# Latent attention loop: key rotation moved from GpSimd to VectorE, and TensorE's order between score units changed

## Chip, cores and metric

One core of one Trainium2 chip. The metric is the device time of one execution of the whole program in microseconds (us). TensorE does matrix products, VectorE and ScalarE elementwise work and reductions, GpSimd elementwise work, SyncE issues DMAs. In the rows they stand as PE (PEld its weight loads), DVE, ACT, POOL and SP.

## What is computed

A decoder of two layers on 32 sequences of 56 tokens of width 256. The change touches one phase of layer 0, the cross attention over a latent context of 1500 rows of width 64 per sequence ("batch"), with 16 heads:

```
kv_rope = kv_c * cos + rotate_half(kv_c) * sin           # 1500 x 64 per batch
scores  = q_r . k_r      (both projected; the kernel folds the weights into the queries)
attn    = softmax(scores)
ctx_c   = attn @ kv_rope                                  # then two output projections
```

Here `rotate_half` swaps the two halves of the 64 columns and negates one; the kernel has the sign in its sine table.

## The kernel before, in words

`latent_attention` first makes the queries of all batches, then runs one loop over the 32 batches (`B`), each engine with its own copy of the loop (`body(b, par)`, where `par` is the parity of `b`) and semaphores between them. The 1500 rows lie as 12 tiles (`KT`) of 125 rows (`KP`). All 16 heads times 56 tokens are 896 columns, held as two halves of 448.

For one batch the work is as follows.

- SyncE loads the raw rows (`raw`, two buffers), spreads the queries, and moves the softmax denominators out and their reciprocals back (`spread_reciprocals`: spread `den` to `den7`, send `rec7`, broadcast it to `rD`).
- GpSimd rotates the rows: `raw*cos` into `rot` (L2395), two half-width products with the sine table into `rot2` (L2397, L2400), their sum into `rot` (L2403), and the low half-precision part of the keys into `kk` (L2409), after ScalarE has written the high part (`high`, L2547). ScalarE also copies `rot` to `kv` (`rows`, L2553), which TensorE reads as the values.
- TensorE transposes the keys in two turns (`turn`, L2442): tiles 0 to 7 of batch b+1 in the last third of body b, tiles 8 to 11 of batch b in its first third. ScalarE copies each turn out of bank 7 (`evacuate`, L2538).
- TensorE makes 12 score units (`scores`, L2477), numbered n = 0 to 11. A unit is three pairs of matmuls into one of three double banks, so unit n waits for the exponential of unit n-3. ScalarE turns each into exponentials in `Pb` (L2588, "exp n").
- TensorE multiplies the exponentials with the values (`values`, L2455), accumulating in bank 6. VectorE adds the 12 tiles of exponentials up into `dsum` (L2638 the first, L2643 the ten others; "sum tt", tt = 1 to 11). TensorE sums `dsum` over the partitions (`denominators`, L2465, bank 7).
- ScalarE copies bank 6 to `pv` (`keep_context`, L2559, at n = 4 of the next body) and bank 7 to `den` (`keep_denominators`, L2565). `pv` is one buffer: `keep_context(b)` waits for `ct_made` to reach b, that is, for VectorE to have used up the previous batch's. VectorE takes the reciprocals (L2624) and scales the context by them (`context`, L2628).

The order on TensorE is written out by hand. Each body has three thirds, g = 0, 1, 2. A third is four score units (4g to 4g+3), then a turn (g = 0 and g = 2), then four tiles of values (g = 0 takes the last four tiles of the batch before), and at g = 0 the denominators of the batch before come after the values. In each engine's loop a wait holds back everything behind it on that engine.

VectorE's order before: sum 1 to 6, the reciprocals of the batch before, sum 7 to 10, the context of the batch before, sum 11. ScalarE's: exp 0 to 3, the second turn's copy, `high` of the next batch, `keep_context` of the batch before, exp 4, `keep_denominators`, exp 5 to 7, `rows` of the next batch, exp 8 to 10, the next batch's first turn copy, exp 11.

Of the kernel before, what the change touches and what calls it, by code (L numbers as in the profile page):

```python
# [2201 lines left out]
def latent_attention(nc, k, t, weights):  # L2202


    with ExitStack() as ctx:
# [62 lines left out]
        with ExitStack() as main:  # L2268
# [16 lines left out]
            raw = sb("raw", [KP, 2, KT, DC], c=main)  # L2285
            rot, rot2 = sb("rot", [KP, 2, KT, DC], c=main), sb("rot2", [KP, KT, DC], c=main)
            kv = sb("kv", [KP, 2, KT, DC], c=main)
# [21 lines left out]
            ones = sb("ones", [KP, DC], c=main)  # L2309
            own_pool = sem("pool")  # L2310
            raw_in = [sem("even_rows_loaded"), sem("odd_rows_loaded")]
            kv_made, kT_done, kT_made = sem("kv_made"), sem("kT_done"), sem("kT_made")
            rotated, kh_made, kl_made = sem("rows_rotated"), sem("kh_made"), sem("kl_made")
# [6 lines left out]

            NTURN = 2

# [3 lines left out]
            with nc.Block() as block:  # L2326
# [51 lines left out]
                @block.gpsimd  # L2378
                def _(pool):
                    s = Steps(pool, own_pool)  # L2380
                    nc.gpsimd.tensor_copy(B16[:, :, 0, :], Bs[:]).then_inc(bh_made, 1)
                    pool.wait_ge(bh_made, 1)
                    nc.gpsimd.tensor_tensor(B16[:, :, 1, :], Bs[:], B16[:, :, 0, :],
                                            ALU.subtract).then_inc(bl_made, 1)
                    pool.wait_ge(tables, 32)
                    Q = DC // 2

                    def body(b, par):
                        r = raw[:, par]

                        pool.wait_ge(raw_in[par], half_count(b, par))
                        if past(b, 2):

                            pool.wait_ge(kv_made, b - 1)
                        s(nc.gpsimd.tensor_tensor(rot[:, par], r, cosK[:], ALU.mult))  # L2395
                        s.settle()
                        s(nc.gpsimd.tensor_tensor(rot2[:, :, 0:Q], r[:, :, Q:DC], sinK[:, :, 0:Q],  # L2397
                                                  ALU.mult))
                        s.settle()
# [3 lines left out]
                        nc.gpsimd.tensor_tensor(rot[:, par], rot[:, par], rot2[:],  # L2403
                                                ALU.add).then_inc(rotated, 1)
                        pool.wait_ge(rotated, b + 1)
                        pool.wait_ge(kh_made, b + 1)
                        if past(b, 2):
                            pool.wait_ge(kT_done, (b - 1) * NTURN)
                        nc.gpsimd.tensor_tensor(halves(par, True), paired(rot[:, par]),  # L2409
                                                halves(par, False), ALU.subtract).then_inc(kl_made, 1)  # L2410
                        pool.wait_ge(kl_made, b + 1)

                    over_tiles(pool, body, 0, s, 3, n=B)

                @block.tensor
                def _(pe):
# [30 lines left out]
                    def values(b, par, tt):  # L2447
                        pe.wait_ge(exp_done, b * KT + (tt // 2 * 2 + 2))
                        if tt == 0:
                            pe.wait_ge(kv_made, b + 1)  # L2450
                        if tt == 0 and past(b, 1):
# [32 lines left out]
                    def body(b, par):  # L2484
# [8 lines left out]
                        for g in range(3):  # L2493
                            if g == 0:
                                pe.wait_ge(kT_made, b * NTURN + 1)
                                pe.wait_ge(spread[par], 4 * half_count(b, par))
                            if g == 2:
                                pe.wait_ge(kT_made, b * NTURN + 2)
                            for pair in (2 * g, 2 * g + 1):
                                for u in range(2):  # L2500
                                    scores(b, par, pair, u)
                            if g == 0:
                                turn(b, par, 1)
                            if g == 2 and live(b + 1, B):
# [19 lines left out]
                def _(act):  # L2524
# [18 lines left out]
                    def high(b, par):  # L2543
                        act.wait_ge(rotated, b + 1)
                        if past(b, 2):
                            act.wait_ge(kT_done, (b - 1) * NTURN)
                        nc.scalar.activation(halves(par, False), paired(rot[:, par]),  # L2547
                                             ACT.Copy).then_inc(kh_made, 1)

                    def rows(b, par):  # L2550
                        if past(b, 2):
                            act.wait_ge(pv_done, (b - 1) * KT)
                        nc.scalar.activation(kv[:, par], rot[:, par], ACT.Copy).then_inc(kv_made, 1)  # L2553

# [12 lines left out]
                    def body(b, par):  # L2567
                        if not live(b, B):
                            keep_queries(0)
                            high(0, 0)  # L2570
                            rows(0, 0)
                            with act.Fori(1, NG - 1) as g:
# [4 lines left out]
                        for n in range(KT):  # L2577
# [27 lines left out]
                def _(dve):  # L2605
# [21 lines left out]
                    def context(b, source):  # L2627
                        nc.vector.tensor_tensor(CT[:, ds(b, 1), :].rearrange("p o n -> p (o n)"),  # L2628
                                                source, rD[:], ALU.mult).then_inc(ct_made, 1)

                    def body(b, par):
                        for tt in range(1, KT):
                            dve.wait_ge(exp_done, b * KT + (tt // 2 * 2 + 2))
# [19 lines left out]
                    over_tiles(dve, body, 0, n=B)  # L2653
                    n = (B - 1) * DR
# [957 lines left out]
```

## Time and profile before

| what | value |
|---|---|
| median of 3 runs | 1872.93 us (1871.71 to 1884.01) |
| the profiled execution | 1873.22 us, of which 1871.5 us are the span of the profile |
| busy over the span | TensorE 1467.8 us (78%), VectorE 1393.7 us (74%), ScalarE 1068.7 us (57%), GpSimd 652.1 us (35%) |
| the latent loop | about 370 us to 981 us of the span |

A timeline row gives the start of an instruction (or of a run of like ones, with their count after the x) in us from the start of the span, the time it covers, the engine, the line of the kernel, what it writes and reads, and in brackets how long the engine had been idle before and what ended that. Successive instructions of an engine overlap a little, so a step is best read from start to start.

### The profile page before, as it was taken

The page shows a single profiled execution, that of the slowest core. Times are in us where ns is not written, and L with a number is a line of the kernel's source. Part 1 is how long each engine was busy: PE and PEld are TensorE (multiplying, and loading weights), DVE is VectorE, ACT ScalarE, POOL GpSimd, SP SyncE. Part 2 cuts the span into 40 slices and gives each one's busy share as a digit, 9 for nine tenths or more (in the row PEclk, how much of TensorE's full clock was granted, in tenths as well). Part 3 has the DMA queues.
Part 4 walks back from the last instruction along what each step waited for, and adds up shares of the span by engine and source line. Part 5 has one row for each costly group of instructions (what it writes and reads, how often), then busy time and mean ns, then how long its engine had stood idle before and what let it go on. Part 6 is the DMA issues. An engine that isn't in the chain of part 4 may idle for free. (4 is left out here: it accounts for less than half of the span.)

```text
span 1871.5 us, 40366 instructions
## 1 busy us (share of the span) xinstructions
PE 1467.8 (78%) x13805; PEld 930.2 (50%) x13820; DVE 1393.7 (74%) x2385; ACT 1068.7 (57%) x1820; POOL 652.1 (35%) x654
## 2 busy tenths in 40 slices
PE   1677776999999999999997466861687759956892
PEld 0455553444444444444447356761465547735782
DVE  6888874799999998888876773326789646667674
ACT  1777763777777776777763342431567435535461
POOL 1222212165555645454510254551333110027242
PEclk9655665999999999999998677985899779958896
DMA  6920000112212121212110153433000010024334
GB/s 157 332 104 1 1 1 33 37 34 56 60 46 69 46 67 49 63 53 64 52 26 2 40 159 121 136 109 109 1 1 0 1 26 1 0 87 135 100 106 157
DMA packets 93389, 123.67 MB, mean 66 GB/s; under 512 B 22945, under 2 KB 74217, under 8 KB 92867
## 3 DMA queue, kind: packets, MB, share of 16 engines
q1 hardware_dynamic: 83395, 98.88, 18.7%
q0 software_dynamic: 7776, 21.28, 3.2%
q10 hardware_dynamic: 2112, 2.10, 0.3%
q8 instruction: 67, 1.10, 0.2%
q14 instruction: 39, 0.32, 0.1%
HBM read 66.85 MB, written 40.30 MB: 57 GB/s over the span
## 5 line engine op out<-in xcount | busy, mean ns | idle before, releaser
L2643 DVE TENSOR_TENSOR lat_dsum<-lat_dsum,lat_Pb 125x896 f32<-125x896 f32 x320 | 481.5, 1505 | 43.0 <-ACT lat_Pb L2588 33.7
L2588 ACT ACTIVATE lat_Pb<-banks 125x896 f32<-125x896 f32 x384 | 329.2, 928 | 145.2 <-PE banks L2477 130.8
L2455 PE MATMUL banks<-lat_Pb,lat_kv 125*64 125x448 f32 x1536 | 306.5, 541 | 0.0
L2477 PE MATMUL banks<-lat_QH,lat_kT 64*125 64x448 f16 x1536 | 247.7, 363 | 5.0 <-DVE lat_QT L2613 2.1
L2477 PEld LDWEIGHTS banks<-lat_QH,lat_kT 64*125 64x125 f16 x1536 | 104.6, 133 | 139.3 <-issue 66.3
L2455 PEld LDWEIGHTS banks<-lat_Pb,lat_kv 125*64 125x64 f32 x1536 | 100.6, 137 | 146.4 <-issue 138.3
L2409 POOL TENSOR_TENSOR lat_kk<-lat_rot,lat_kk 125x768 f16<-125x768 f32 x32 | 66.9, 2090 | 265.3 <-ACT lat_kk L2547 265.3
L2978 POOL DMA_INDIRECT sent_outputs<-moe_yb,moe_yidx x98 | 99.4, 1014 | 135.9 <-ACT moe_yb L3235 107.7
L2477 PE MATMUL banks<-lat_QL,lat_kT 64*125 64x448 f16 x768 | 136.0, 351 | 0.0
L3116 PE MATMUL banks<-moe_w2d,moe_gT 88*128 (+3 forms) x780 | 106.1, 288 | 22.6 <-DVE moe_gT L3453 15.6
L3116 PEld LDWEIGHTS banks<-moe_w2d,moe_gT 88*128 88x128 f16 (+1 forms) x780 | 77.5, 103 | 39.6 <-issue 27.0
L3441 DVE COPY moe_xTb<-banks 128x1024 f16<-128x1024 f16 x49 | 33.8, 689 | 83.8 <-PE banks L3083 45.9
L2970 POOL DMA_INDIRECT sent_rows<-moe_arena,moe_idx x64 | 70.8, 1106 | 53.0 <-DVE moe_idx L3382 33.9
L3033 PE MATMUL banks<-moe_xTb,moe_w2i 128*88 128x256 f16 (+1 forms) x588 | 77.0, 282 | 13.0 <-DVE moe_xTb L3441 13.0
L2403 POOL TENSOR_TENSOR lat_rot<-lat_rot 125x768 f32<-125x768 f32 x32 | 80.0, 2501 | 2.5
L2395 POOL TENSOR_TENSOR lat_rot<-lat_raw,lat_cosK 125x768 f32<-125x768 f32 x32 | 69.7, 2179 | 29.0 <-DMA lat_raw<-in_ctx_dram 23.8
L3033 PEld LDWEIGHTS banks<-moe_xTb,moe_w2i 128*88 (+1 forms) x588 | 63.6, 115 | 19.6 <-issue 14.9
L1270 POOL TENSOR_TENSOR bit_vv<-bit_vf,bit_one 128x256 f16<-128x256 f32 x16 | 11.0, 689 | 163.8 <-PE banks L1557 153.3
L3194 ACT ACTIVATE moe_gT<-banks 88x512 f32<-88x512 f32 x37 | 21.9, 591 | 76.5 <-PE banks L3033 57.6
L2477 PEld LDWEIGHTS banks<-lat_QL,lat_kT 64*125 64x125 f16 x768 | 52.7, 134 | 10.3
L2638 DVE TENSOR_TENSOR lat_dsum<-lat_Pb 125x896 f32<-125x896 f32 x32 | 53.5, 1673 | 3.6 <-ACT lat_Pb L2588 3.6
L2397 POOL TENSOR_TENSOR lat_rot<-lat_raw,lat_sinK 125x384 f32<-125x384 f32 x32 | 54.5, 1704 | 2.5
(446 smaller groups left out, 3256.8 us busy)
## 6 DMA issues: line engine op xcount, KB each, us to landing
moe_xb<-sent_rows SPq DMA_DIRECT2D x49, 257.0 KB
lat_raw<-in_ctx_dram SPq DMA_DIRECT2D x32, 375.0 KB
sent_rows<-zero SPq DMA_DIRECT2D x1, 7453.0 KB, 49.0
lat_QH<-lat_QT SPq DMA_DIRECT2D x64, 112.0 KB, 2.9
lat_QL<-lat_QT SPq DMA_DIRECT2D x64, 112.0 KB, 5.0
lat_rD<-lat_reciprocals SPq DMA_DIRECT2D x62, 112.0 KB, 2.8
moe_arena<-sent_outputs SPq DMA_DIRECT2D x12, 512.0 KB, 6.5
sent_rows<-zero SPq DMA_DIRECT2D x1, 5140.0 KB, 65.1
```

The costliest lines, as they stand in the source:

```text
L2395: s(nc.gpsimd.tensor_tensor(rot[:, par], r, cosK[:], ALU.mult))
L2397: s(nc.gpsimd.tensor_tensor(rot2[:, :, 0:Q], r[:, :, Q:DC], sinK[:, :, 0:Q], ALU.mult))
L2403: nc.gpsimd.tensor_tensor(rot[:, par], rot[:, par], rot2[:], ALU.add).then_inc(rotated, 1)
L2409: nc.gpsimd.tensor_tensor(halves(par, True), paired(rot[:, par]), halves(par, False), ALU.subtract).then_inc(kl_made, 1)
L2455: ins = nc.tensor.matmul(ps[u * DC:(u + 1) * DC, 6, 0:8 * T], kv[:, par, tt, :], Pb[:, tile_slot(tt, par), u, :], start=tt == 0, stop=tt = ...
L2477: ins = nc.tensor.matmul(ps[0:KP, n % 3 * 2 + q, 0:8 * T], kT[rows, par, 2 * pair + low, 0:KP], Q[rows, par, 8 * u:8 * u + 8, :].rearrange ...
L2588: nc.scalar.activation(Pb[:, slot:slot + 2, u, :], ps[0:KP, n % 3 * 2:n % 3 * 2 + 2, 0:8 * T], ACT.Exp, scale=1.0 / QSCALE).then_inc(exp_d ...
L2643: ins = nc.vector.tensor_tensor(dsum[:, par], dsum[:, par], Pb[:, tile_slot(tt, par)], ALU.add)
L2970: nc.gpsimd.indirect_dma_start(xg[:, :], bass.IndirectOffsetOnAxis(ap=idx[:, c, i:i + 1], axis=0), rows[:, i, :], None).then_inc((sent0, s ...
L2978: nc.gpsimd.indirect_dma_start(ytok[:, :], bass.IndirectOffsetOnAxis(ap=yidx[:, n, h:h + 1], axis=0), yb[:, n % 3, h, :], None).then_inc(y ...
L3033: ins = nc.tensor.matmul(ps[0:FP, dst, j * BN:(j + 1) * BN], w[:, u, c, j * FP:(j + 1) * FP], rhs(v, c), start=a + c == 0, stop=a == 2 and ...
L3116: ins = nc.tensor.matmul(dst, gT2[:, n % 2, u, j, h * P:(h + 1) * P], w[:, v, j, :], start=a + j == 0, stop=last and not (gated and b < 0))
```

## The change

GpSimd rotates only the rows of batches 0 and 1, before the loop. For the others VectorE does it: it makes the three products of batch b+2 at the end of body b (`row_products`), adds them straight into `kv` after sum 3 of body b+1 (`rotated_rows`; the values of two batches earlier must have been used), and makes the low part after sum 7 (`low`). ScalarE's copy `rows` is gone; `high` reads `kv` and comes after exp 5 instead of exp 3. On TensorE the two turns and the denominators are put ahead of the last score unit of a third instead of behind the third, and the denominators move from g = 0 to g = 1. ScalarE keeps the denominators after exp 7 and VectorE takes their reciprocals after sum 9. The context of batch b-2 is scaled after sum 3 of body b, behind the rotation's sum; `keep_context` on ScalarE is unchanged. After the loop VectorE scales the context of batch 30 before its last checks.

The diff, cut to its core:

```
                 @block.tensor
-                            for pair in (2 * g, 2 * g + 1):
-                                for u in range(2):
-                                    scores(b, par, pair, u)
+                            for pair, u in ((2 * g, 0), (2 * g, 1), (2 * g + 1, 0)):
+                                scores(b, par, pair, u)
                             if g == 0:
                                 turn(b, par, 1)
+                            if g == 1 and past(b, 1):
+                                denominators(b - 1, (par + 1) % 2)
                             if g == 2 and live(b + 1, B):
                                 turn(b + 1, (par + 1) % 2, 0)
+                            scores(b, par, 2 * g + 1, 1)
                             for tt in range(4 * g - 4, 4 * g):
...
-                            if g == 0 and past(b, 1):
-                                denominators(b - 1, (par + 1) % 2)
                 @block.scalar
                             if n == 3:
                                 evacuate(b, par, 1)
-                                if live(b + 1, B):
-                                    high(b + 1, (par + 1) % 2)
-                            if n == 7 and live(b + 1, B):
-                                rows(b + 1, (par + 1) % 2)
-                            if n == 4 and past(b, 1):
+                            if n == 5 and live(b + 1, B):
+                                high(b + 1, (par + 1) % 2)
+                            if n == 7 and past(b, 1):
                                 keep_denominators(b - 1)
                 @block.vector
+                    def kept_context(b):
+                        dve.wait_ge(pv_kept, b + 1)
+                        dve.wait_ge(rec_in, 32 * b + 32)
+                        context(b, pv[:])
+                    def row_products(b, par):
+                        r = raw[:, par]
+                        dve.wait_ge(raw_in[par], half_count(b, par))
+                        dve.wait_ge(rotated, b)
+                        nc.vector.tensor_tensor(rot[:], r, cosK[:], ALU.mult)
+                        nc.vector.tensor_tensor(rot2[:, :, 0:Q], r[:, :, Q:DC], sinK[:, :, 0:Q], ALU.mult)
+                        nc.vector.tensor_tensor(rot2[:, :, Q:DC], r[:, :, 0:Q], sinK[:, :, Q:DC], ALU.mult)
+                    def rotated_rows(b, par):
+                        dve.wait_ge(products_made, 3 * b - 3)
+                        dve.wait_ge(pv_done, (b - 1) * KT)
+                        nc.vector.tensor_tensor(kv[:, par], rot[:], rot2[:], ALU.add).then_inc(rotated, 1)
+                    def low(b, par):
+                        dve.wait_ge(kh_made, b + 1)
+                        nc.vector.tensor_tensor(halves(par, True), paired(kv[:, par]),
+                                                halves(par, False), ALU.subtract).then_inc(kl_made, 1)
                     def body(b, par):
...
-                            if tt == 6 and past(b, 1):
+                            if tt == 3 and past(b, 1) and live(b + 1, B):
+                                rotated_rows(b + 1, other)
+                            if tt == 3 and past(b, 2):
+                                kept_context(b - 2)
+                            if tt == 7 and past(b, 1) and live(b + 1, B):
+                                low(b + 1, other)
+                            if tt == 9 and past(b, 1):
                                 reciprocals(b - 1)
-                            if tt == KT - 2 and past(b, 1):
-                                dve.wait_ge(pv_kept, b)
-                                dve.wait_ge(rec_in, 32 * b)
-                                context(b - 1, pv[:])
+                        if live(b + 2, B):
+                            row_products(b + 2, par)
+                    kept_context(B - 2)
```

On GpSimd, the loop over all batches becomes `for b in range(2)` with the same five instructions, the sum written to `kv[:, b]`.

## Rows read from the trace of the kernel before

**Rows 1.** The page's granted TensorE clock in 40 slices of the span

```profile
PEclk9655665999999999999998677985899779958896
```

**Rows 2.** ScalarE's copies of the context, one per batch: durations, first and last start

```profile
L2559 ACT ACTIVATE lat_pv<-banks x31: 543/543/547, 392.7 to 965.6; 128x448 f32<-128x448 f32 x31
```

**Rows 3.** Timeline of TensorE, one body from its g = 1 values on

```profile
819.56 3.23 PE L2455 MATMUL banks<-lat_Pb,lat_kv 125*64 125x448 f32 x16
...
825.30 0.63 PE L2442 MATMUL banks<-id,lat_kk 125*64 125x125 f16 x16
...
831.53 0.41 PE L2442 MATMUL banks<-id,lat_kk 125*64 125x125 f16 x8
831.78 3.18 PE L2455 MATMUL banks<-lat_Pb,lat_kv 125*64 125x448 f32 x16
834.79 0.92 PE L2465 MATMUL banks<-lat_dsum,lat_ones 125*64 125x448 f32 x4
835.64 0.40 PE L2477 MATMUL banks<-lat_QH,lat_kT 64*125 64x448 f16 x2
...
838.29 3.23 PE L2455 MATMUL banks<-lat_Pb,lat_kv 125*64 125x448 f32 x16
```

**Rows 4.** Timeline, all engines, of an earlier batch, where TensorE waits for VectorE

```profile
604.20 2.53 DVE L2638 TENSOR_TENSOR lat_dsum<-lat_Pb 125x896 f32<-125x896 f32 x1
604.42 0.97 PE L2465 MATMUL banks<-lat_dsum,lat_ones 125*64 125x448 f32 x4 [0.79 <-DVE lat_dsum L2643]
```

**Rows 5.** The sums on VectorE over the loop (group by line: total busy us, mean ns)

```profile
L2643 DVE TENSOR_TENSOR lat_dsum<-lat_dsum,lat_Pb 125x896 f32<-125x896 f32 x320 | 481.5, 1505 | 43.0 <-ACT lat_Pb L2588 33.7
```

**Rows 6.** Timeline of TensorE near the loop's end: four score units and the turn behind

```profile
959.63 0.40 PE L2477 MATMUL banks<-lat_QH,lat_kT 64*125 64x448 f16 x2
959.87 0.35 PE L2477 MATMUL banks<-lat_QL,lat_kT 64*125 64x448 f16 x2
960.06 0.54 PE L2477 MATMUL banks<-lat_QH,lat_kT 64*125 64x448 f16 x4
...
961.85 0.35 PE L2477 MATMUL banks<-lat_QH,lat_kT 64*125 64x448 f16 x2
962.13 0.41 PE L2442 MATMUL banks<-id,lat_kk 125*64 125x125 f16 x8
```

**Rows 7.** Timeline, exp 4 and what follows it on ScalarE and TensorE

```profile
836.61 0.92 ACT L2588 ACTIVATE lat_Pb<-banks 125x896 f32<-125x896 f32 x1 [0.98 <-PE banks L2477]
837.42 0.54 ACT L2565 ACTIVATE lat_den<-banks 128x448 f32<-128x448 f32 x1
837.58 0.13 PEld L2477 LDWEIGHTS banks<-lat_QH,lat_kT 64*125 64x125 f16 x2 [0.43 <-ACT lat_Pb L2588]
837.85 2.54 ACT L2588 ACTIVATE lat_Pb<-banks 125x896 f32<-125x896 f32 x3
```

**Rows 8.** Timeline, exponentials and the sums that wait for them, GpSimd idle

```profile
954.37 2.54 ACT L2588 ACTIVATE lat_Pb<-banks 125x896 f32<-125x896 f32 x3 [1.16 <-PE banks L2477]
...
956.22 2.22 DVE L2643 TENSOR_TENSOR lat_dsum<-lat_dsum,lat_Pb 125x896 f32<-125x896 f32 x2 [0.75 <-ACT lat_Pb L2588]
958.74 1.09 DVE L2643 TENSOR_TENSOR lat_dsum<-lat_dsum,lat_Pb 125x896 f32<-125x896 f32 x1 [0.30 <-ACT lat_Pb L2588]
959.75 0.62 DVE L2628 TENSOR_TENSOR lat_QT<-lat_pv,lat_rD 128x448 f32 x1
```

**Rows 9.** Timeline: a reciprocal and the context behind it, then the loop's tail

```profile
616.64 0.19 DVE L2624 RECIPROCAL lat_rec<-lat_den 128x7 f32 x1
...
621.94 0.63 DVE L2628 TENSOR_TENSOR lat_QT<-lat_pv,lat_rD 128x448 f32 x1 [0.72 <-DMA lat_rD<-lat_reciprocals]
...
971.90 0.40 PE L2477 MATMUL banks<-lat_QH,lat_kT 64*125 64x448 f16 x2
...
979.37 0.27 DVE L2657 TENSOR_SCALAR lat_good<-lat_rec 128x217 f32<-128x217 f32 x1
...
981.51 2.96 DVE L2665 RECIPROCAL lat_rD<-banks 128x448 f32<-128x448 f32 x1 [1.04 <-PE banks L2465]
```

More of the change, by code:

```diff
@@ L2285, in latent_attention @@
             raw = sb("raw", [KP, 2, KT, DC], c=main)
-            rot, rot2 = sb("rot", [KP, 2, KT, DC], c=main), sb("rot2", [KP, KT, DC], c=main)
+            rot, rot2 = sb("rot", [KP, KT, DC], c=main), sb("rot2", [KP, KT, DC], c=main)
             kv = sb("kv", [KP, 2, KT, DC], c=main)
@@ L2309, in latent_attention @@
             ones = sb("ones", [KP, DC], c=main)
-            own_pool = sem("pool")
+            own_pool, products_made = sem("pool"), sem("row_products_made")
             raw_in = [sem("even_rows_loaded"), sem("odd_rows_loaded")]
-            kv_made, kT_done, kT_made = sem("kv_made"), sem("kT_done"), sem("kT_made")
+            kT_done, kT_made = sem("kT_done"), sem("kT_made")
             rotated, kh_made, kl_made = sem("rows_rotated"), sem("kh_made"), sem("kl_made")
@@ L2319, in latent_attention @@
                 sem("good_reduced"), sem("good_counted"))
-            NTURN = 2
+            NTURN, Q = 2, DC // 2
             def past(i, least=0):
@@ L2385, in _ @@
                     pool.wait_ge(tables, 32)
[L2386 to L2396, printed above, removed]
+                    for b in range(2):
+                        r = raw[:, b]
+                        pool.wait_ge(raw_in[b], 16)
+                        if b:
+                            pool.wait_ge(rotated, 1)
+                        s(nc.gpsimd.tensor_tensor(rot[:], r, cosK[:], ALU.mult))
                         s(nc.gpsimd.tensor_tensor(rot2[:, :, 0:Q], r[:, :, Q:DC], sinK[:, :, 0:Q],
                                                   ALU.mult))
-                        s.settle()
                         s(nc.gpsimd.tensor_tensor(rot2[:, :, Q:DC], r[:, :, 0:Q], sinK[:, :, Q:DC],
@@ L2402, in body @@
                         s.settle()
-                        nc.gpsimd.tensor_tensor(rot[:, par], rot[:, par], rot2[:],
-                                                ALU.add).then_inc(rotated, 1)
+                        nc.gpsimd.tensor_tensor(kv[:, b], rot[:], rot2[:], ALU.add).then_inc(rotated, 1)
                         pool.wait_ge(rotated, b + 1)
                         pool.wait_ge(kh_made, b + 1)
[L2407 to L2413, printed above, removed]
+                        nc.gpsimd.tensor_tensor(halves(b, True), paired(kv[:, b]), halves(b, False),
+                                                ALU.subtract).then_inc(kl_made, 1)
                 @block.tensor
@@ L2449, in values @@
                         if tt == 0:
-                            pe.wait_ge(kv_made, b + 1)
+                            pe.wait_ge(rotated, b + 1)
                         if tt == 0 and past(b, 1):
@@ L2546, in high @@
                             act.wait_ge(kT_done, (b - 1) * NTURN)
-                        nc.scalar.activation(halves(par, False), paired(rot[:, par]),
+                        nc.scalar.activation(halves(par, False), paired(kv[:, par]),
                                              ACT.Copy).then_inc(kh_made, 1)
[L2550 to L2553, printed above, removed]
                     def keep_context(b):
@@ L2570, in body @@
                             high(0, 0)
-                            rows(0, 0)
                             with act.Fori(1, NG - 1) as g:
@@ L2629, in context @@
                                                 source, rD[:], ALU.mult).then_inc(ct_made, 1)
+                    def kept_context(b):
[6 more added lines that the diff above has]
+                        dve.wait_ge(rotated, b)
+                        nc.vector.tensor_tensor(rot[:], r, cosK[:], ALU.mult).then_inc(products_made, 1)
+                        nc.vector.tensor_tensor(rot2[:, :, 0:Q], r[:, :, Q:DC], sinK[:, :, 0:Q],
+                                                ALU.mult).then_inc(products_made, 1)
+                        nc.vector.tensor_tensor(rot2[:, :, Q:DC], r[:, :, 0:Q], sinK[:, :, Q:DC],
+                                                ALU.mult).then_inc(products_made, 1)
+                    def rotated_rows(b, par):
+                        dve.wait_ge(products_made, 3 * b - 3)
+                        dve.wait_ge(pv_done, (b - 1) * KT)
+                        nc.vector.tensor_tensor(kv[:, par], rot[:], rot2[:], ALU.add
+                                                ).then_inc(rotated, 1)
+                    def low(b, par):
+                        dve.wait_ge(kh_made, b + 1)
+                        nc.vector.tensor_tensor(halves(par, True), paired(kv[:, par]),
+                                                halves(par, False), ALU.subtract).then_inc(kl_made, 1)
                     def body(b, par):
+                        if not live(b, B):
+                            return
+                        other = (par + 1) % 2
                         for tt in range(1, KT):
@@ L2645, in body @@
                             ins.then_inc(summed, 1)
-                            if tt == 6 and past(b, 1):
-                                reciprocals(b - 1)
-                            if tt == KT - 2 and past(b, 1):
-                                dve.wait_ge(pv_kept, b)
-                                dve.wait_ge(rec_in, 32 * b)
-                                context(b - 1, pv[:])
-                    over_tiles(dve, body, 0, n=B)
+                            if tt == 3 and past(b, 1) and live(b + 1, B):
[5 more added lines that the diff above has]
+                            if tt == 9 and past(b, 1):
+                                reciprocals(b - 1)
+                        if live(b + 2, B):
+                            row_products(b + 2, par)
+                    over_tiles(dve, body, 1, n=B)
+                    kept_context(B - 2)
                     n = (B - 1) * DR
```

## Prediction

> **What bounds the kernel now.** I read the page's slices first, for the phases and the granted clock: in the loop's slices TensorE holds its upper level, 2.4 GHz, with a 9 in each of them up to the last [rows 1]. So a matmul has one price there and the loop can be read as a pattern. Next the period. ScalarE's copy of the context runs once per body, and 31 of them span 965.6-392.7 = 572.9 us, 30 periods of 19.10 us [rows 2]. Then TensorE's timeline of one body. From values to the like values it takes 838.29-819.56 = 18.73 us [rows 3], with no gap in which TensorE waits long. Earlier bodies add a wait of up to 0.79 us before the denominators, for VectorE's last sum [rows 4], which makes the mean 19.10. VectorE is late there because a sum takes 1505 ns in the mean [rows 5] against 1.09 us where GpSimd is idle [rows 8]; one of 2.53 us stands in [rows 4]. So TensorE's own order is the floor, and VectorE, slowed beside GpSimd, adds 0.37 us per body. That is all the change can win from VectorE's relief, however many busy microseconds go.
>
> **TensorE's order, part by part.** A score unit is three pairs of matmuls, 0.19 us a pair (959.87 to 960.06); entering the scores costs 0.05 more (959.63 to 959.87 is 0.24) and leaving them 0.09 (961.85 to 962.13 is 0.28) [rows 6]. Twelve pairs with both edges are 2.41 us (with 0.1885 for a pair, before rounding). The same third takes 2.50 in [rows 6] and 838.29-835.64 = 2.65 us in [rows 3]: up to 0.24 us is the fourth unit's wait for the exponential three units back, with its restart. Four tiles of values cost 834.79-831.78 = 3.01 us between a turn and the denominators, and the denominators 835.64-834.79 = 0.85 for two pairs of 0.375, so leaving this kind of matmul for scores costs 0.10 [rows 3]. Values between scores then cost 3.01+0.05+0.10 = 3.16. A turn of 8 transposes costs 831.78-831.53 = 0.25 us, one of 16 about 0.47 (its record is 0.22 longer) [rows 3].
>
> In the new order each third is three units, the inserted work, one unit, values. Three units: 9 x 0.1885 + 0.14 = 1.84; the last unit 0.71. So g = 0 is 1.84+0.25+0.10+0.71+3.16 = 6.06 us; g = 1, with denominators of 0.75+0.05, is 6.61; g = 2 is 6.28. The sum is 18.95 us against 18.73: six more edge pairs of about 0.15 cost as much as the three waits give back, and a little more. I take the turn's exit to be the denominators' 0.10, the nearest row; its bounds are nothing and the 0.15 of a full edge, 0.2 us per body either way.
>
> The Trainium skill, TensorEngine Tiling (Array Packing), section Key Properties, says that a change of tiling mode (not only of tile) drains TensorE. Scores use 64 rows and the rest 125, and the rows' 0.05 to 0.10 us per edge agree. Without that rule one would book the three waits as pure gain.
>
> **VectorE and ScalarE.** VectorE loses nothing of its 11 sums (1.09 us each, 2.22-1.09 = 1.13 from one to the next) [rows 8]. It gains one sum and one low part of 768 columns and three products of 768, 384, 384. The trace has no such operation on VectorE: by its rows of 448 and 896 columns, 0.62 and 1.09 us [rows 8], 768 columns are 0.96 and 384 are 0.55 (bounds for 768: those two rows). That is 4.0 us, and with 12.3 of sums, the context and the reciprocal 17.1 us per body, under the period: VectorE isn't filled. ScalarE loses the 0.9 us copy and isn't filled either. GpSimd leaves the loop. The two ramps for which it still works (batches 0 and 1) I cost at nothing: batch 0's low part was ready long before the loop, and batch 1's turn comes over 5 us after the exponentials that its high part follows. SyncE's order is unchanged; the raw rows have more than half a body of slack, and its queue is released by the reciprocals as before.
>
> **The wait that the change builds.** `keep_context` of batch b-1 stands on ScalarE ahead of exp 4 of body b and waits until the context of batch b-2 is made. Before, VectorE had made that one in body b-1, so the wait cost nothing. Now it is made in the same body b, after sum 3 and behind the rotation's sum. Exp 4 to 11, `high` and both copies are queued behind `keep_context`. I walk one body. Times are from the start of g = 0.
>
> - Exp 0 starts 0.98 after the third's first unit (836.61 against 835.64), the next ones 0.81 apart [rows 3, 7]. Exp 3 starts at 3.41, and VectorE's sum 2, which waits for it, 1.04 later (0.92 and 0.12 of latency: 956.22 is 1.85 after the first of two exponentials) [rows 8]: 4.45. Sum 3 at 5.58. The rotation's sum at 6.59 (1.01 after a sum) [rows 8]; its own wait, for the values of g = 0, ends before, at about 6.25. The context at 7.47 (0.96 less the overlap of 0.08), done at 8.09.
> - `keep_context` starts at 8.21 and exp 4 at 8.64 (0.43 after a 0.54 copy: 837.42 to 837.85) [rows 7]. From the start of g = 1 (6.06) that is 2.58, where it used to be 0.98. The last unit of g = 1 may start 0.97 after exp 4 (836.61 to 837.58) [rows 7], at 3.55; the order alone would have it at 1.84+0.80+0.10 = 2.74. **First stall: 0.81 us.**
> - Exp 5 follows at 3.39 from the start of g = 1, `high` at 4.20, exp 6 at 4.90 (0.70 for `high`'s 768 columns, between the 0.43 and 0.81 that copies of 448 and 896 take to the next start [rows 7], which bound it), exp 7 at 5.71. Sum 6 waits for exp 7: 4.90+1.85 = 6.75. Sum 7 at 7.88, the low part at 8.89, done at 9.85. The turn of g = 2 waits for it: 9.98. g = 2 starts at 6.61+0.81 = 7.42 and would turn at 9.26. **Second stall: 0.72 us.** The denominators, once the late link, now have over 6 us to spare.
> - The sums 8 to 11 and the products end at 2.3 us into the next body, before exp 1 is there (2.7), so nothing more accumulates, and nothing is caught up.
>
> The period is 18.95+0.81+0.72 = 20.48 us. In which body it holds: from 2 to 30; body 1 has no context to wait for (18.97), and body 31 no rotation and no turn. Sum over the 30 periods: 29 x 20.48 + 18.97 = 612.9 us against 572.9, +40.0. For bodies 0 and 31, +0.2.
>
> **The tail.** The reciprocal of batch 30 now comes after sum 9, about 4.9 us into the last third, and the context waits for the DMAs behind it, 621.94-616.64 = 5.3 us [rows 9]: it runs at 10.2 to 10.85, three short checks (979.37 to 980.5, about 1.1 us) follow, and the reciprocal of L2665 starts near 11.9 after the last third's start. Before it was 981.51-971.90 = 9.6 [rows 9]: +2.3.
>
> **Sum.** 40.0+0.2+2.3 = +42.5. The profiled execution took 1873.2 us, 0.3 from the median of the runs shown, so both lead to 1916 us. The links of the chain are good to about 0.3 us a period, 9 us in all.
>
> **Rivals.**
>
> - One stall only (the turn's). If the low part is ready in time (a quicker `high`, or exp 7 not held as I think), the period is 19.76 and the time 1916-29 x 0.72 = 1895 us. For it: the two stalls are worked out in series and the second hangs on eleven links. Against: each link has its row. Chance 0.15.
> - The clock. Each body now has two idle stretches of TensorE of 0.75 us. In the earlier bodies, stretches of 0.79 [rows 4] left the granted clock at its upper level [rows 1]. If it falls to 1.2 GHz in some bodies, each such fall costs two to three microseconds by the time a third of scores takes at half rate (2.65 against twice that); eight of them give 1936. Chance 0.1.
> - Not slower: the context is made before `keep_context` wants it. It decides at 1.22 us after the start of g = 1 (2.74-0.97-0.43-0.12); I put it at 2.03. If VectorE is 0.8 us earlier, both stalls go, the period is 18.95, and the time is 1873-(572.9-29 x 18.95-18.97)+2.5 = 1871 us. For it: VectorE is much less busy. Against: sum 2 waits for exp 3, whose time TensorE and ScalarE set, and the wait for the values holds the rotation's sum until 6.25, so the chain can win 0.3 us at most. Chance 0.1.
> - Clearly faster: edges and waits both cheap, VectorE's relief counted in full. Period 18.73 less three waits of 0.24, 18.0: 1873-1.1 x 30+2.5, or 1843 us. The Trainium skill, SBUF — State Buffer, section Who interferes with whom, has VectorE and GpSimd lock each other out of one shared port pair, and here sums of 2.53 against 1.09 us agree; as a rule for the time it speaks for this case. Against: TensorE's floor and the wait built. Chance 0.05.
>
> The forecast has 0.6. The range, from 1892 (under one stall) to 1932 (0.6 us more per period), leaves out about 0.2. A measurement of this kernel tells about 1% from no change. The stalls, one or two, and the clock give slower; one stall at its low end touches 1%. Slower 0.84, within 1% 0.11, faster 0.05.
>
> **What would show it.** ScalarE's L2559 waiting for VectorE's context, 1 to 2 us each; exp 4 starting some 2.5 us after the first score unit of g = 1; 30 copies of the context 20.4 us apart; TensorE idle before the fourth unit of g = 1 and before the 16 transposes, and not before the denominators; sums of 1.09 us throughout. It is wrong if those copies are 19 us apart, or if TensorE waits in other places.

## The result and the profile after

The changed kernel takes 1918.24 us in the median of 4 runs (1915.18 to 1918.77), the kernel before 1872.32 us beside it. The ratio is 1.024, 95% interval 1.020 to 1.028. The forecast was 1916 us.

The page of the kernel after, its slices and its costliest groups in the loop (columns as before: count, busy us, mean ns, idle before and its releaser):

```profile
PEclk9665657999999999999998867995799879958896
...
L2652 DVE TENSOR_TENSOR lat_dsum<-lat_dsum,lat_Pb 125x896 f32<-125x896 f32 x320 | 350.8, 1096 | 116.7 <-ACT lat_Pb L2570 105.1
L2570 ACT ACTIVATE lat_Pb<-banks 125x896 f32<-125x896 f32 x384 | 329.3, 926 | 129.0 <-PE banks L2465 128.8
```

VectorE is relieved as the change meant it to be: a sum takes 1096 ns in the mean, against 1505 in [rows 5]. It is also idle far more, 116.7 us before those sums against 43.0, waiting for exponentials. The granted clock stays at its upper level through the loop, as in [rows 1]. So the time was not lost to VectorE's work, nor to the clock.

ScalarE's copy of the context, which answers to [rows 2] (durations in ns, first and last start):

```profile
L2542 ACT ACTIVATE lat_pv<-banks x31: 543/543/544, 393.2 to 1005.5; 128x448 f32<-128x448 f32 x31
```

The waits of the latent phase, 340 to 1030 us (who waited for whom, total us, times, longest):

```profile
ACT lat_pv L2542 <- DVE lat_QT L2608: 99.2, 30, 3.4
PEld banks L2465 <- ACT lat_Pb L2570: 64.7, 63, 1.5
...
PE banks L2465 <- ACT lat_Pb L2570: 19.8, 30, 0.7
PE banks L2430 <- DVE lat_kk L2634: 19.5, 29, 0.7
```

The 31 copies span 1005.5-393.2 = 612.3 us, where the forecast had 612.9 and the kernel before 572.9. The waits name the links. The copy waits 30 times for VectorE's context (it used to wait for TensorE's values); TensorE waits 30 times for an exponential and 29 times for the low part, 0.7 us each, and never for a sum before the denominators.

One period in the timeline, ScalarE, VectorE and TensorE, each engine's rows together. The third g = 0 starts at 610.29 and g = 1 at 616.35:

```profile
611.27 3.35 ACT L2570 ACTIVATE lat_Pb<-banks 125x896 f32<-125x896 f32 x4 [2.85 <-PE banks L2465]
618.41 0.54 ACT L2542 ACTIVATE lat_pv<-banks 128x448 f32<-128x448 f32 x1 [3.31 <-DVE lat_QT L2608]
618.85 1.72 ACT L2570 ACTIVATE lat_Pb<-banks 125x896 f32<-125x896 f32 x2
...
614.75 2.22 DVE L2652 TENSOR_TENSOR lat_dsum<-lat_dsum,lat_Pb 125x896 f32<-125x896 f32 x2 [0.54 <-ACT lat_Pb L2570]
616.88 0.95 DVE L2629 TENSOR_TENSOR lat_kv<-lat_rot 125x768 f32<-125x768 f32 x1
617.75 0.62 DVE L2608 TENSOR_TENSOR lat_QT<-lat_pv,lat_rD 128x448 f32 x1
...
605.86 0.63 PE L2430 MATMUL banks<-id,lat_kk 125*64 125x125 f16 x16 [0.67 <-DVE lat_kk L2634]
610.29 0.40 PE L2465 MATMUL banks<-lat_QH,lat_kT 64*125 64x448 f16 x2
616.35 0.40 PE L2465 MATMUL banks<-lat_QH,lat_kT 64*125 64x448 f16 x2
619.81 0.40 PE L2465 MATMUL banks<-lat_QH,lat_kT 64*125 64x448 f16 x2 [0.64 <-ACT lat_Pb L2570]
```

Read from 610.29: sum 2 at 4.46 us, the rotation's sum at 6.59, the context at 7.46, `keep_context` at 8.12, exp 4 at 8.56, the fourth unit of g = 1 at 9.52. The forecast had 4.45, 6.59, 7.47, 8.21, 8.64 and 9.61.

### The profile page after: what moved, and what is told of

Same layout as the page of the kernel before. It is cut to its first block and busy times, and to the rows that moved or that the text cites. A ratio compares the mean times of both kernels' runs of the same rounds, so it can differ in the third digit from the quotient of the medians.

```text
span 1916.0 us, 40187 instructions
## 1 busy us (share of the span) xinstructions
PE 1476.1 (77%) x13805; PEld 933.7 (49%) x13820; DVE 1355.4 (71%) x2535; ACT 1042.5 (54%) x1788; POOL 342.3 (18%) x504
## 5 line engine op out<-in xcount | busy, mean ns | idle before, releaser
L2652 DVE TENSOR_TENSOR lat_dsum<-lat_dsum,lat_Pb 125x896 f32<-125x896 f32 x320 | 350.8, 1096 | 116.7 <-ACT lat_Pb L2570 105.1
L3047 PEld LDWEIGHTS banks<-moe_xTb,moe_w2i 128*88 (+1 forms) x588 | 63.0, 114 | 19.7 <-issue 14.8
L2542 ACT ACTIVATE lat_pv<-banks 128x448 f32<-128x448 f32 x31 | 16.8, 543 | 100.7 <-DVE lat_QT L2608 99.2
L3097 PE MATMUL banks<-id,moe_xb 128*128 128x128 f16 x392 | 32.5, 230 | 26.7 <-DMA moe_xb<-sent_rows 26.7
L2526 ACT ACTIVATE lat_kT<-banks 128x1000 f16<-128x1000 f16 x64 | 52.8, 825 | 0.0
L2410 PE MATMUL banks<-lat_cols,lat_A 128*128 (+1 forms) x128 | 51.2, 562 | 1.1 <-DVEq L2587 1.1
L3224 ACT ACTIVATE moe_uT<-banks,moe_bug 128x256 f32<-128x256 f32 x56 | 23.5, 470 | 51.0 <-PE banks L3047 26.5
```

The source lines that it names most:

```text
L2410: ins = nc.tensor.matmul(ps[:, j % 4, 0:GN], A[:, c, 2 * j:2 * j + 2, :].rearrange("p h d -> p (h d)"), cols[:, c, ds(g * GN, GN)], start= ...
L2526: nc.scalar.activation(kT[:, par, 8 * c:8 * c + n, 0:KP], ps[:, 7, :].bitcast(F16)[:, 0:n * KS].rearrange("p (n k) -> p n k", n=n)[:, :, 0 ...
L2652: ins = nc.vector.tensor_tensor(dsum[:, par], dsum[:, par], Pb[:, tile_slot(tt, par)], ALU.add)
L3047: ins = nc.tensor.matmul(ps[0:FP, dst, j * BN:(j + 1) * BN], w[:, u, c, j * FP:(j + 1) * FP], rhs(v, c), start=a + c == 0, stop=a == 2 and ...
L3097: ins = nc.tensor.transpose(bank[:, a, h * P:(h + 1) * P], xb[:, b % XB, h, a * P:(a + 1) * P], id16[:])
```

## The experiments

The runs fell on different chips. On the chip of the first four experiments the kernel before takes 1847.38 us, 25 us less than in the result above, so times are compared as ratios and periods. In the traces most of that difference lies behind the loop: from its last check to the end of the span these four take 861 to 867 us, the kernel before 885 in its first trace.

**Taking the two stalls apart.** Four kernels, each the changed one with one or two edits. Exchange of the context and the rotation's sum:

```
+                            if tt == 3 and past(b, 2):
+                                kept_context(b - 2)
                             if tt == 3 and past(b, 1) and live(b + 1, B):
                                 rotated_rows(b + 1, other)
-                            if tt == 3 and past(b, 2):
-                                kept_context(b - 2)
```

> The changed kernel with two statements of VectorE exchanged: after sum 3 the context of batch b-2 comes ahead of the rotation's sum. Theory (keep_context waits for that context, and the low part for exp 7): exp 4 starts 1.7 us after g = 1 begins instead of 2.6, the fourth unit of g = 1 no longer waits, the turn of g = 2 still does (about 0.65 us); period 19.6 us, time about 1894 us. Rival (VectorE's 4 us of added work per body is what costs): the same work in another order, so no change, 1918 us. Rival (TensorE's six added mode edges cost): no change, 1918 us.

Measured: ratio to the kernel before 1.011 (1.006 to 1.016), against 1.024 for the full change in the result above. From its waits between 400 and 970 us:

```profile
ACT lat_pv L2542 <- DVE lat_QT L2608: 71.5, 29, 2.5
...
PE banks L2430 <- DVE lat_kk L2634: 15.6, 29, 0.6
```

The row of TensorE waiting on its matmuls for an exponential is gone; the turn's wait for the low part stays. ScalarE's copy still waits 2.5 us (counted from its last instruction), but that no longer costs TensorE anything. Its copies span 979.8-392.6 = 587.2 us, a period of 19.57 where 19.6 was expected. One of the two stalls went, and the wait of the other is a little shorter (15.6 us in 29 times is 0.54, against 0.67), because exp 4 and all behind it still start late, but less late.

The low part after sum 5:

```
-                            if tt == 7 and past(b, 1) and live(b + 1, B):
+                            if tt == 5 and past(b, 1) and live(b + 1, B):
                                 low(b + 1, other)
```

> The changed kernel with the low part after sum 5 instead of sum 7. Theory: the turn of g = 2 no longer waits, the fourth unit of g = 1 still waits 0.8 us; period about 19.7 us, time about 1897 us. Both rivals (VectorE's load, TensorE's edges): no change, 1918 us.

Measured: ratio 1.013 (1.008 to 1.018). The other stall went and the first stayed, by its waits between 400 and 970 us. Its copies span 590.8 us, 19.69 a period where about 19.7 was expected.

```profile
ACT lat_pv L2542 <- DVE lat_QT L2608: 96.7, 29, 3.4
...
PE banks L2465 <- ACT lat_Pb L2570: 19.2, 29, 0.7
```

Both edits at once:

> Both exchanges at once. Theory: no stall is left in the loop, the period is TensorE's own order, 18.95 us, and the time about 1875 us; the two gains add up. Rival (VectorE's load): 1918 us. Rival (edges cost more than 0.15 us each): the period stays clearly above 19.1 us without any wait of TensorE for another engine.

Measured: ratio 1.000 (0.995 to 1.005). The copies span 569.5 us, 18.98 us a period:

```profile
L2542 ACT ACTIVATE lat_pv<-banks x31: 543/543/544, 391.5 to 961.0; 128x448 f32<-128x448 f32 x31
```

A second buffer for the kept context instead, VectorE's order untouched:

```
-            rD, pv = sb("rD", [P, 8 * T], c=main), sb("pv", [P, 8 * T], c=main)
+            rD, pv = sb("rD", [P, 8 * T], c=main), sb("pv", [P, 2, 8 * T], c=main)
...
-                        if past(b, 1):
-                            act.wait_ge(ct_made, b)
-                        nc.scalar.activation(pv[:], ps[:, 6, 0:8 * T], ACT.Copy)
+                        if past(b, 2):
+                            act.wait_ge(ct_made, b - 1)
+                        nc.scalar.activation(pv[:, par], ps[:, 6, 0:8 * T], ACT.Copy)
```

> The changed kernel, VectorE's order untouched, with two buffers for the kept context, so that keep_context waits for the context of one batch earlier. Theory: the first stall goes, and with it the second (exp 7 is 0.8 us earlier and more); period 18.95 us, time about 1875 us. If the two stalls are independent: the second stays, about 1895 us. Rivals: 1918 us.

Measured: ratio 1.000 (0.995 to 1.005). The copies now wait for TensorE's values alone, and both stalls are gone although the low part still comes after sum 7 (waits between 400 and 940 us; the copies span 568.6 us, 18.95 a period):

```profile
ACT lat_pv L2542 <- PE banks L2443: 39.4, 28, 1.4
```

So the second stall isn't a cost of its own. It is the first one's delay of exp 4 handed on through exp 7 to the sums behind; either breaking the handing on or removing its head is enough. The load rival falls with all four runs: the VectorE work was the same in each, 4 us a body more than before.

**The two parts of the change by themselves.** VectorE's part, with TensorE's order, denominators and context as before (here the low part is after sum 5):

```
-                            for pair, u in ((2 * g, 0), (2 * g, 1), (2 * g + 1, 0)):
-                                scores(b, par, pair, u)
+                            for pair in (2 * g, 2 * g + 1):
+                                for u in range(2):
+                                    scores(b, par, pair, u)
...
-                            if tt == 3 and past(b, 2):
-                                kept_context(b - 2)
+                            if tt == KT - 2 and past(b, 1):
+                                kept_context(b - 1)
```

> One part of the change alone: VectorE rotates (products at the body's end, the rotation's sum after sum 3, the low part after sum 5), GpSimd is out of the loop and the copy of rows is gone, but TensorE's order, the denominators, the reciprocals and the context stand as in the kernel before. Theory: the period is the late one of the kernel before, 18.73 us in every body, with no wait before the denominators; 0.37 us less than its mean over 30 periods, so 11 us faster than the kernel before, ratio 0.994. Rival (VectorE's added 4 us cost by themselves): no faster than the kernel before.

Measured: ratio 0.998 (0.9965 to 0.9995). The period came as forecast; here are TensorE's rows of one body, to be laid beside [rows 3]:

```profile
651.09 0.92 PE L2453 MATMUL banks<-lat_dsum,lat_ones 125*64 125x448 f32 x4
...
660.34 0.63 PE L2430 MATMUL banks<-id,lat_kk 125*64 125x125 f16 x16
...
666.57 0.41 PE L2430 MATMUL banks<-id,lat_kk 125*64 125x125 f16 x8
666.82 3.18 PE L2443 MATMUL banks<-lat_Pb,lat_kv 125*64 125x448 f32 x16
669.83 0.92 PE L2453 MATMUL banks<-lat_dsum,lat_ones 125*64 125x448 f32 x4
```

From denominators to denominators 18.74 us, and 3.01 us of values ahead of them, so no wait for VectorE. The same holds over the whole loop: the copies of the context span 561.2 us, 18.71 a period. But the gain in time is 3.7 us (1861.8 against 1865.52), not 11. The period was right and the comparison wasn't.

The order part, with GpSimd rotating as before:

```
+                            if tt == 1 and past(b, 2):
+                                kept_context(b - 2)
-                            if tt == 6 and past(b, 1):
+                            if tt == 9 and past(b, 1):
                                 reciprocals(b - 1)
-                            if tt == KT - 2 and past(b, 1):
...
-                                context(b - 1, pv[:])
```

> The other part alone: TensorE's new order (turns and denominators ahead of the third's last score unit) with GpSimd rotating as before; the context of batch b-2 is made after sum 1, where ScalarE doesn't wait for it. Theory: period 18.95 us, six more mode edges against three waits of the fourth unit; no wait for VectorE before the denominators in spite of GpSimd, since they come later; 0.15 us a period less than the mean before, 2 us more in the tail: ratio 0.999. Rival (the inserted work hides the waits for nothing): period 18.0 to 18.3 us, ratio 0.985 to 0.99.

Measured: ratio 1.015 (1.013 to 1.017), a miss. The waits between 450 and 920 us say why:

```profile
ACT lat_pv L2559 <- DVE lat_QT L2628: 60.4, 24, 3.2
...
DVE lat_QT L2628 <- DMA lat_rD<-lat_reciprocals: 50.9, 24, 2.8
```

I had put the context so early that it waited for the reciprocals' DMA, and ScalarE waited for it again: the same chain with another head. TensorE waited for an exponential 28 times in the loop, most often for 0.5 us. To tell this from an effect of GpSimd, the same kernel with two buffers and the context after sum 3:

> e7_order_part_alone (TensorE's new order, GpSimd rotating) with two buffers for the kept context and the context made after sum 3, so that neither ScalarE nor VectorE waits for the reciprocals' DMA. Theory (e7 lost its 0.5 us a body to keep_context waiting for a context that waited for that DMA): period 18.95 us, ratio 0.997 to 1.003. Rival (GpSimd beside VectorE makes the new order slow by itself): period stays at 19.5 us, ratio about 1.015.

Measured: ratio 1.001 (0.999 to 1.003). GpSimd works and the sums are as slow as before (the group of the sums, then the copies of the context), and yet the period is TensorE's own order, since the denominators come later:

```profile
L2648 DVE TENSOR_TENSOR lat_dsum<-lat_dsum,lat_Pb 125x896 f32<-125x896 f32 x317 | 477.0, 1505 | 29.9 <-ACT lat_Pb L2588 21.1
```

```profile
L2559 ACT ACTIVATE lat_pv<-banks x31: 544/545/547, 393.4 to 962.0; 128x448 f32<-128x448 f32 x31
```

568.6 us over 30 periods are 18.95. The order part alone is worth nothing. By itself the new order is 0.22 us a body longer than the old one at its best (18.95 against 18.73): it saves three waits of the fourth unit, and pays for six more changes between the scores, which use 64 rows of TensorE, and the other matmuls, which use 125 ("changes of mode" from here on). What made up for that here is that the denominators no longer wait for a slowed sum.

**GpSimd put back beside the rotation.** The VectorE part alone, and per body five GpSimd instructions of the old shapes on tiles of their own:

```
+                    def beside(b, par):
+                        pool.wait_ge(exp_done, b * KT + 4)
+                        s(nc.gpsimd.tensor_tensor(g1[:], sinK[:], cosK[:], ALU.mult))
...
+                    over_tiles(pool, beside, 0, s, 5, n=B)
```

> The kernel of e6_vector_part_alone with the five GpSimd instructions of the old loop put back on tiles of their own, paced by exp 3 of each body, so that nothing waits for them. Theory (the two engines slow each other whatever the data): sums on VectorE go from 1.09 us back to about 1.5 us in the mean where the five run, VectorE needs over 19 us a body together with the rotation, and the time is above the kernel before, ratio 1.01 to 1.03. Rival (the old slowness came from waits on shared tiles): sums stay at 1.09 us, the time equals e6_vector_part_alone.

Measured: ratio 1.074 (1.071 to 1.076), above what I expected. The sums went back to 1495 ns in the mean though they share no tile with GpSimd. The group of the sums, a stretch of the timeline, and a row of the waits between 450 and 1020 us:

```profile
L2669 DVE TENSOR_TENSOR lat_dsum<-lat_dsum,lat_Pb 125x896 f32<-125x896 f32 x310 | 463.3, 1495 | 18.4 <-ACT lat_Pb L2587 10.9
```

```profile
749.59 5.20 DVE L2669 TENSOR_TENSOR lat_dsum<-lat_dsum,lat_Pb 125x896 f32<-125x896 f32 x2
755.58 2.21 DVE L2669 TENSOR_TENSOR lat_dsum<-lat_dsum,lat_Pb 125x896 f32<-125x896 f32 x2
...
748.68 2.54 POOL L2413 TENSOR_TENSOR lat_g<-lat_g,lat_g2x 125x768 f32<-125x768 f32 x1
```

```profile
ACT lat_kk L2552 <- DVE lat_kv L2646: 93.1, 25, 7.9
```

Two sums take 5.20 us beside GpSimd's and 2.21 us after. The excess over the expectation is in part again a chain: `high` on ScalarE waits for the rotation's sum, which stands behind the slowed sums, and every later exponential stands behind `high`. TensorE then stands still for up to 6.1 us at a time, and behind such a wait its granted clock falls to the lower level, 1.2 GHz: a row of four matmuls, 0.54 us before the wait, is 0.95 behind it. Two such rows, and then the loop in this kernel and in the VectorE part alone (stretch, its length, busy us and count of PE, PEld, DVE, ACT and POOL, granted clock, DMA share, GB/s):

```profile
757.39 0.63 PE L2482 MATMUL banks<-lat_QH,lat_kT 64*125 64x448 f16 x2 [4.81 <-ACT lat_Pb L2587]
...
758.19 0.95 PE L2482 MATMUL banks<-lat_QH,lat_kT 64*125 64x448 f16 x4
```

```profile
392.00:1096.00 704.00, 598.97 (x4444) 272.67 (x4444) 664.32 (x544) 399.42 (x511) 311.66 (x151) 0.93 0.18 44
```

```profile
389.00:950.00 561.00, 559.25 (x4442) 253.18 (x4440) 476.95 (x539) 393.73 (x510) 0.00 (x0) 1.00 0.22 56
```

For the same matmuls TensorE is busy 599.0 us against 559.3. So of the 142 us that the loop is longer, about 105 are idle time of TensorE and about 40 are its lower clock, which the expectation didn't have.

**A version that beats both.** Four groups of three score units with 4, 2, 4 and 2 tiles of values behind them. Turns and denominators stay next to values (the cut leaves out the new places on ScalarE and VectorE):

```
+                        for g in range(4):
...
+                            for n in range(3 * g, 3 * g + 3):
+                                scores(b, par, n // 2, n % 2)
+                            if g == 0:
+                                turn(b, par, 1)
+                            if g == 2 and live(b + 1, B):
+                                turn(b + 1, (par + 1) % 2, 0)
+                            for tt in ((), (0, 1), (2, 3, 4, 5), (6, 7))[g]:
+                                values(b, par, tt)
+                            if g == 0 and past(b, 1):
+                                for tt in range(KT - 4, KT):
+                                    values(b - 1, (par + 1) % 2, tt)
+                                denominators(b - 1, (par + 1) % 2)
```

> A version meant to beat both: four groups of three score units instead of three of four, with values of 4, 2, 4 and 2 tiles behind them, turns and denominators next to values, so that no unit waits for an exponential inside its group and TensorE changes mode 8 times a body instead of 6 or 12. VectorE rotates (sum after sum 1, low part after sum 2, products and reciprocals after sum 7, context after sum 11). Theory: period 18.73 less 0.67 of waits plus two edge pairs of 0.15, 18.36 us, ratio to the kernel before 0.988. Rival (VectorE, now at 17 of 18.4 us, binds): period 18.7 to 19, with TensorE waiting for the low part or the denominators for sum 11.

Measured: ratio 0.993 (0.992 to 0.994), 1853.11 against 1865.52 us. TensorE's rows of one body:

```profile
631.11 0.92 PE L2453 MATMUL banks<-lat_dsum,lat_ones 125*64 125x448 f32 x4
633.80 1.72 PE L2443 MATMUL banks<-lat_Pb,lat_kv 125*64 125x448 f32 x8
...
637.30 0.63 PE L2430 MATMUL banks<-id,lat_kk 125*64 125x125 f16 x16
...
642.72 1.72 PE L2443 MATMUL banks<-lat_Pb,lat_kv 125*64 125x448 f32 x8
646.22 0.41 PE L2430 MATMUL banks<-id,lat_kk 125*64 125x125 f16 x8
...
649.48 0.92 PE L2453 MATMUL banks<-lat_dsum,lat_ones 125*64 125x448 f32 x4
```

The period is 18.37 us (forecast 18.36), TensorE waits for no exponential, low part or sum, and the copies of the context (392.5 to 943.6) give the same over 30 periods. Here too the loop's gain of about 22 us by the traces shows as 12 us in the runs.

**Where the missing 8 to 10 us are.** The two kernels above had the periods forecast but won less against the kernel before. A second trace of that one, on a chip other than those of the experiments so far:

> The kernel before, unchanged, for a second trace. e6_vector_part_alone and e8_threes had the periods forecast (18.73 and 18.37 us in every body) but won 9 us less than their loops should against the kernel before. Theory: the kernel before is not one pattern; how often GpSimd's instructions fall beside VectorE's last sums differs from execution to execution, so the wait before the denominators does, and here the mean of the periods may be anything from 18.75 to 19.1 us. Rival: the loop repeats the 19.10 us of the first trace, and the missing 9 us lie outside the loop.

The total was the same, 573.0 us over 30 periods, so the rival's number came out, and the theory's range took in 19.1 only as its end. Here are the copies of the context in that trace:

```profile
L2559 ACT ACTIVATE lat_pv<-banks x31: 543/544/547, 393.3 to 966.3; 128x448 f32<-128x448 f32 x31
```

But the pattern was not the same. TensorE's waits for a sum before the denominators, in the first trace of the kernel before and then in this one:

```profile
PE banks L2465 <- DVE lat_dsum L2643: 7.0, 13, 2.4
```

```profile
PE banks L2465 <- DVE lat_dsum L2643: 7.2, 7, 2.9
```

Thirteen waits in the one and seven in the other, the seven all in bodies in which the first trace has one too, but of other lengths. They are not all short. One of the first trace is 2.40 us long, and two of the second are 2.53 and 2.92 us. Behind each of the three TensorE ran for a little over 3 us at the lower clock. Here are the long wait of the first trace and the stretch behind it (columns as above, the granted clock third from the end):

```profile
720.94 1.02 PE L2465 MATMUL banks<-lat_dsum,lat_ones 125*64 125x448 f32 x4 [2.40 <-DVE lat_dsum L2643]
```

```profile
722.00:725.00 3.00, 3.00 (x18) 1.84 (x20) 2.97 (x2) 1.54 (x3) 2.92 (x2) 0.50 0.01 4
```

The body with that wait takes 22.7 us. From the next one on, at 741 us, every body takes 18.3 to 18.8 us to the loop's end. In the second trace that begins at 630 us, behind bodies of 21.1 and 21.5 us. The second trace also has four bodies without a wait, of 18.7 to 18.95 us, between 435 and 510 us, before the waits come back. So the kernel before has bodies with the waits and bodies without, and its loop's time depends on how many it has of each. On the chip of those two experiments its runs took 1861.56 to 1872.16 us, the version in threes 1851.79 to 1853.88, but the VectorE part alone 1857.56 to 1868.17, so a spread of 10 us isn't the mark of GpSimd either. A kernel before whose loop was better in those runs than in either trace would fit, but no trace of it was taken on that chip, and the difference stays open.

## Why the prediction was right, point by point

- **TensorE's own order, 18.95 us.** Right. With the stalls gone it is what remains (18.98 and 18.95 us), with GpSimd or without. The turn's exit, taken as the denominators' 0.10, showed as turns of 0.56 and 0.34 against 0.47 and 0.25, 0.09 us.
- **What the kernel before loses, 0.37 us a body.** The size was right, since it is the measured mean less the floor, and its source only in part. The waits before the denominators are up to 2.40 us and not 0.79, and their 7.0 us are less than the 11.0 us by which the 30 periods exceed 18.73. Part of the rest is the lower clock behind the longest: four score units there took 725.89-721.89 = 4.00 us, against 2.65 in [rows 3].
- **The wait for the context in the same body, 0.81 us.** Right in place, a little long: the copy follows the context at 0.04 us after its end and not at 0.12, so exp 4 is 0.08 earlier and the stall 0.72 us.
- **The low part after exp 7, 0.72 us.** Right (the turn waits 0.67 by the row, about 0.7 with its restart). The rival of one stall fell. The run that moves the low part prices the second stall at 20.41-19.69 = 0.72 us a period. The exchange of the context and the rotation's sum gave 20.41-19.57 = 0.84, the first stall and the little that it took off the second.
- **VectorE's added work hidden.** Right: its rotation, 0.95 and 0.55 us an instruction, lies in time in which it waited for exponentials. The exception is the one that the forecast had in its chain: the rotation's sum ahead of the context.
- **The tail, +2.3 us.** The reciprocals' DMA path was 4.96 us this time, not 5.3, and the last reciprocal started 1022.50-1011.08 = 11.4 us after the last third began, against 9.6: +1.8.
- **The sum.** Up to the loop's last check the trace is 1027.9-986.9 = 41.0 us longer, where 42.5 were forecast. Another 3.5 us of the profiled execution lie in phases that the change doesn't touch (the span less that check, 888.1 against 884.6), which the sum didn't have. So part of the closeness of 1916 to 1918 is luck.
- **What would show it.** I had named waits of 1 to 2 us on the copy; the row says 3.3, because it counts from the end of ScalarE's last instruction. With two buffers the same copy starts 0.11 us after g = 1 (658.12 against 658.01), here 2.06, so the delay is 1.95.
- **The other rivals.** The clock held through stalls of 0.7 us, at 1.00 in the mean over the loop. The price that this rival had for a fall, two to three us, was too high: the one after 720.94 cost 4.00-2.65 = 1.35 us. That the context could be ready in time fell for the order as written, and held once two instructions were exchanged. Cheap edges fell with the order part alone.

## What to carry to other kernels

When an engine's work is moved within a loop, look at the waits that were left alone: a single buffer whose release moves from the body before into the same body turns a wait that cost nothing into the head of a chain. On engines in program order one late instruction can be paid at several consumers behind it (here 0.72 us and 0.73). Price a reordering on TensorE by counting changes of mode as well as waits, and choose a grouping in which the wait can't arise (three units for three banks) rather than one that fills it.

## What the runs showed of the hardware beyond this

A change between the scores' shape (64 rows) and the others' (125 rows), in either direction, costs TensorE about 0.15 us: 0.09 to 0.10 before the other kind starts and 0.05 at its first pair. Starting from the measured 18.73 us with 6 changes a body, periods worked out with that price for 8 and for 12 changes were met within 0.03 us. Between transposes and values, both of 125 rows, the turn of 8 took 0.25 us, against 0.34 in front of scores. VectorE's sums of two tensors slow from 1.1 to 2.6 us beside GpSimd instructions that share no data with them. That much was expected.

Two things were not. The kernel with both engines busy took two different courses in two executions, with thirteen waits or with seven and the same total. And the granted clock, which stayed at 1.00 in the mean through the changed kernel's loop with its 58 stalls of up to 0.7 us, fell to 0.50 for a little over 3 us behind each of the three waits of 2.40 to 2.92 us in the two traces of the kernel before.
